# A decoder layer on one core: the next batch's load and transposes moved, identity products in TensorE's waits, work lists laid out anew

## What is computed

```python
x = x + attn(layernorm(x))                  # per batch:
    xs = x shifted by one token
    k, v, r = (x * tm + xs * (1 - tm)) @ W.T, for each of three tm and W; r = sigmoid(r)
    y = (r * layernorm(_wkv(decay, first, k, v)) * ln_g + ...) @ Wo.T
x = x + _wkv(w, u, layernorm(x), ctx)
x = x + ffn(layernorm(x))                   # 1408 inner channels
    h = silu(x @ gate.T * gate_s) * (x @ up.T * up_s)
    y = h @ down.T * down_s
```

## Time and profile before

| | |
|---|---|
| median of three runs | 597.04 us |
| the profiled execution | 597.9 us |
| its span, first to last instruction | 596.1 us |
| mean granted clock of TensorE, share of full speed | 0.958 |
| TensorE busy | 535.3 us, 90% |
| VectorE busy | 458.4 us, 77% |
| ScalarE busy | 350.4 us, 59% |
| GpSimd busy | 52.1 us, 9% |

### The profile page before, as it was taken

How to read it: one execution, slowest core, us unless ns; L and a number is a source line. 1 busy time by engine, 2 the same in 40 slices (tenths; PEclk the granted TensorE clock), 3 DMA queues, 4 the chain that set the end, 5 groups by cost and what they waited for, 6 DMA issues and landing times.

```text
span 596.1 us, 7498 instructions
## 1 busy us (share of the span) xinstructions
PE 535.3 (90%) x2658; PEld 383.0 (64%) x2658; DVE 458.4 (77%) x742; ACT 350.4 (59%) x551; POOL 52.1 (9%) x155
## 2 busy tenths in 40 slices
...
GB/s 304 412 304 369 322 0 0 2 36 35 4 138 2 0 1 0 11 43 19 90 124 1 0 1 0 2 54 18 1 124 2 1 54 36 1 1 36 1 36 38
DMA packets 14264, 39.08 MB, mean 66 GB/s; under 512 B 1233, under 2 KB 1233, under 8 KB 14033
## 3 DMA queue, kind: packets, MB, share of 16 engines
...
...
## 4 chain that ended last, share of the span: by engine, by line
PE 74%; DMA 10%; DVE 7%; issue 3%; SPq 2%; ACT 2%; POOL 2%; DVEq 0%; POOLq 0%; ACTq 0%
PE gu L653 27%; PE bank L569 20%; PE dacc L583 12%; PE bank L631 9%; PE bank L558 5%; DMA down_words<-in_down_t 4%; DMA gate_words<-in_gate_t 3%; DMA t_mixv<-in_x 3%; PE bank L608 1%; DVE t_otile L1076 1%; DVE t_slot L880 1%; DVE t_stats L906 1%; DVE t_z L872 1%; DVE t_st L1018 1%; ACT L676 1%
## 5 line engine op out<-in xcount | busy, mean ns | idle before, releaser
L653 PE MATMUL gu<-t_z4h,t_gate 128*128 128x256 f32 x352 | 93.1, 297 | 1.3 <-DVE t_h L1055 0.7
L653 PE MATMUL gu<-t_z4l,t_gate 128*128 128x256 f32 x352 | 88.5, 284 | 0.0
L653 PE MATMUL gu<-t_z4h,t_up 128*128 128x256 f32 x352 | 87.2, 281 | 0.0
L653 PE MATMUL gu<-t_z4l,t_up 128*128 128x256 f32 x352 | 87.2, 281 | 0.0
L805 ACT ACTIVATE t_h<-gu,t_fsc 128x256 f32<-128x256 f32 x88 | 40.8, 472 | 55.5 <-PE gu L653 50.4
L583 PE MATMUL dacc<-t_down,t_hh 128*128 128x512 f32 x176 | 71.0, 403 | 0.8 <-DVE t_otile L1076 0.8
L653 PEld LDWEIGHTS gu<-t_z4h,t_gate 128*128 128x128 f32 x352 | 67.4, 191 | 6.7 <-issue 3.2
L653 PEld LDWEIGHTS gu<-t_z4l,t_gate 128*128 128x128 f32 x352 | 67.4, 192 | 2.5 <-issue 1.7
L583 PE MATMUL dacc<-t_down,t_hl 128*128 128x512 f32 x176 | 68.9, 391 | 0.0
L676 ACT ACT_TABLE_LOAD x52 | 66.7, 1283 | 1.7 <-PEq L1114 0.7
L653 PEld LDWEIGHTS gu<-t_z4h,t_up 128*128 128x128 f32 x352 | 66.6, 189 | 0.0
(11 more groups left out here) (128 smaller groups left out, 931.1 us busy)
## 6 DMA issues: line engine op xcount, KB each, us to landing
...
gate_words<-in_gate_t SPq DMA_DIRECT2D x1, 2816.0 KB, 17.2
up_words<-in_up_t SPq DMA_DIRECT2D x1, 2816.0 KB, 24.9
t_gate<-gate_words SPq DMA_DIRECT2D x1, 2816.0 KB, 16.4
down_words<-in_down_t SPq DMA_DIRECT2D x1, 2816.0 KB, 23.7
```

The costliest lines, as they stand in the source:

```text
L653: last = pe.matmul(gu[u % 2][:, side, :], as_read(w[:, k, i * P:(i + 1) * P], exact), as_read(part[:, k, hf * HALF:(hf + 1) * HALF], exact ...
```

## The change

Four things. First, `vecs` is loaded behind the two halves of x of batch 0. Second, the copy of the down weights becomes a step of `SP_STEPS` (`copy2.0`), and there x of batch 1 is loaded behind the up weights and ahead of the load of the down weights; the orders of the later loads differ too. Third, a new step `warm` of TensorE issues two products of the identity with itself into a bank that nobody reads at that time; there are eight such steps in the prologue. Fourth, all the lists of steps are new. In batch 0 and 1 `return2.0` now stands ahead of `turn1.1`, `rw0.0` to `rw3.0` ahead of `share_k0.1`, `v3.0` behind `r1.0`, and TensorE's `flag.0` between `r0.1` and `r1.1`. Later `k0`, `k1`, `v0` of batch 2 stand ahead of `wo.1`, `wo.2` ahead of `k0.3`, and `r3.2`, `r3.3` behind `y.1`, `y.2`.

```diff
     PE_STEPS = steps("""
-        turn1.0 k0.0 k1.0 v0.0 v1.0 k2.0 k3.0 v2.0 v3.0 r0.0 r1.0 r2.0 r3.0 turn2.0 turn1.1 k0.1
-        return2.0 k1.1 v0.1 v1.1 wo.0 turn3.0 r0.1 r1.1 r2.1 r3.1 k2.1 k3.1 v2.1 v3.1 y.0 flag.0
-        turn4_0.0 turn4_1.0 up0.0 up1.0 turn2.1 up2.0 up3.0 up4.0 down0.0 return2.1 up5.0 down1.0 up6.0
-        turn1.2 up7.0 wo.1 k0.2 k1.2 v0.2 k2.2 k3.2 up8.0 up9.0 v1.2 v2.2 up10.0 down2.0 up11.0 down3.0
...
-        down16.0 down17.0 up20.0 up21.0 r2.2 r3.2 down18.0 down19.0 down20.0 down21.0 y.1 turn4_0.1
-        turn4_1.1 up0.1 turn2.2 up1.1 up2.1 up3.1 return2.2 down0.1 down1.1 up4.1 turn1.3 up5.1 wo.2
...
-        down16.1 down17.1 down18.1 down19.1 y.2 down20.1 down21.1 r2.3 turn4_0.2 r3.3 up0.2 turn4_1.2
...
+        turn1.0 k0.0 k1.0 v0.0 v1.0 k2.0 k3.0 v2.0 r0.0 r1.0 v3.0 r2.0 r3.0 turn2.0 return2.0 warm0.0
+        warm1.0 turn1.1 warm2.0 warm3.0 k0.1 v0.1 k1.1 v1.1 wo.0 warm4.0 warm5.0 warm6.0 turn3.0 r0.1
+        flag.0 warm7.0 r1.1 r2.1 r3.1 k2.1 k3.1 v2.1 v3.1 y.0 turn4_0.0 turn4_1.0 up0.0 up1.0 turn2.1
+        up2.0 up3.0 up4.0 return2.1 up5.0 down0.0 turn1.2 up6.0 down1.0 k0.2 k1.2 v0.2 wo.1 k2.2 k3.2
...
+        down18.0 down19.0 down20.0 down21.0 y.1 r3.2 turn4_0.1 turn4_1.1 turn2.2 up0.1 up1.1 up2.1
+        return2.2 up3.1 wo.2 up4.1 turn1.3 up5.1 down0.1 k0.3 k1.3 v0.3 v1.3 k2.3 k3.3 down1.1 up6.1
...
+        down19.1 down20.1 down21.1 y.2 r3.3 turn4_0.2 turn4_1.2 up0.2 turn2.3 up1.2 up2.2 up3.2
...
     DVE_STEPS = steps("""
         stat1_0.0 stat1_1.0 norm0.0 norm1.0 mixk0.0 mixk1.0 mixk2.0 mixk3.0 mixv0.0 mixv1.0 mixv2.0
-        front0.0 mixv3.0 mixr0.0 front1.0 nv0.0 den0.0 num0.0 mixr1.0 part0.0 nv1.0 den1.0 num1.0 fin0.0
...
-        part3.0 fin2.0 fin3.0 stat2_0.0 stat2_1.0 stat1_0.1 stat1_1.1 norm2.0 norm3.0 norm0.1 norm1.1
-        mixk0.1 mixk1.1 mixk2.1 mixk3.1 mixv0.1 mixv1.1 front0.1 rw0.0 rw1.0 rw2.0 mixv2.1 mixv3.1 rw3.0
...
+        mixv3.0 mixr0.0 front0.0 front1.0 mixr1.0 mixr2.0 nv0.0 den0.0 num0.0 mixr3.0 part0.0 nv1.0
+        den1.0 num1.0 part1.0 fin0.0 fin1.0 front2.0 front3.0 den2.0 nv2.0 num2.0 part2.0 nv3.0 den3.0
+        num3.0 part3.0 fin2.0 fin3.0 stat2_0.0 stat2_1.0 stat1_0.1 norm2.0 norm3.0 stat1_1.1 norm0.1
+        norm1.1 rw0.0 rw1.0 rw2.0 rw3.0 mixk0.1 mixk1.1 mixk2.1 mixk3.1 mixv0.1 mixv1.1 mixv2.1 mixv3.1
...
+        mixv2.2 mixv3.2 front0.2 den0.2 nv0.2 num0.2 front1.2 rest1.0 prod5.0 rest2.0 x1_0.1 x1_1.1
+        x1_2.1 x1_3.1 part0.2 norm4.1 prod6.0 norm5.1 den1.2 mixr0.2 fin0.2 front2.2 nv1.2 prod7.0
...
+        norm3.2 prod1.1 stat1_0.3 rw0.2 rw1.2 rw2.2 rw3.2 norm0.3 stat1_1.3 x1_0.2 prod2.1 rest0.1
+        prod3.1 norm1.3 x1_1.2 x1_2.2 x1_3.2 rest1.1 norm4.2 norm5.2 mixk0.3 mixk1.3 mixk2.3 mixk3.3
...
     SP_STEPS = steps("""
-        words1.0 words2.0 xload0.1 xload1.1 ctx2.0 ctx3.0 ctx0.1 ctx1.1 rload0.1 rload1.1 xload0.2
...
+        copy2.0 words1.0 xload0.1 xload1.1 words2.0 ctx2.0 ctx3.0 rload0.1 xload0.2 xload1.2 rload1.1
+        xload0.3 ctx0.1 out0.0 ctx1.1 ctx2.1 ctx3.1 out1.0 ctx0.2 out2.0 xload1.3 out3.0 rload0.2 ctx1.2
...
         @block.sync
         def _(sp):
-            sp.dma_start(vecs[:, :, :], vecs_in.rearrange("p (n c) -> p n c", c=C)).then_inc(vec_in, 16)
...
             load_x(0, 0)
             load_x(0, 1)
+            sp.dma_start(vecs[:, :, :], vecs_in.rearrange("p (n c) -> p n c", c=C)).then_inc(vec_in, 16)
...
             copy_words(*ffn_w[0])
             copy_words(*ffn_w[1])
             load_words(*ffn_w[0])
-            copy_words(*ffn_w[2])
...
+                elif s == "copy2":
+                    copy_words(*ffn_w[2])
...
+                elif kind(s) == "warm":
+
+                    for _ in range(2):
+                        pe.matmul(gu[1][:, 0, 0:P], ident[:, :], ident[:, :], start=True, stop=True)
```

More of the change, by code:

```diff
@@ L124, in decoder_layer @@
[L124 to L125 removed]
+        share_v3.0 share_r0.0 share_r1.0 share_r2.0 front0.0 share_r3.0 front1.0 part0.0 part1.0
+        front2.0 front3.0 tanh0.0 tanh1.0 part2.0 tanh2.0 part3.0 tanh3.0 weigh0.0 weigh1.0 norm2.0
+        norm3.0 norm0.1 norm1.1 rw0.0 rw1.0 rw2.0 rw3.0 share_k0.1 share_k1.1 share_k2.1 share_k3.1
@@ new lines, in decoder_layer @@
+        share_v0.1 share_v1.1 share_v2.1 share_v3.1 share_r0.1 share_r1.1 share_r2.1 share_r3.1 weigh2.0
+        front0.1 front1.1 weigh3.0 weigh4.0 part0.1 part1.1 sq4.0 sq5.0 norm4.0 norm5.0 xfront0.0
+        xfront1.0 weigh5.0 xpart0.0 xpart1.0 xfront2.0 xfront3.0 tanh0.1 tanh1.1 tanh2.1 tanh3.1
+        xpart2.0 xpart3.0 front2.1 front3.1 sq6.0 sq7.0 norm6.0 norm7.0 z4_0_0.0 z4_0_1.0 part2.1
+        z4_1_0.0 z4_1_1.0 part3.1 silu0.0 silu1.0 silu2.0 high0.0 norm2.1 norm3.1 silu3.0 high1.0
@@ new lines, in decoder_layer @@
+        high7.0 xpart1.1 silu18.0 silu19.0 xfront2.1 xfront3.1 high8.0 high9.0 silu20.0 silu21.0
+        xpart2.1 high10.0 tanh0.2 xpart3.1 tanh1.2 tanh2.2 sq6.1 sq7.1 norm6.1 tanh3.2 z4_0_0.1 norm7.1
+        z4_0_1.1 z4_1_0.1 z4_1_1.1 silu0.1 norm2.2 norm3.2 silu1.1 silu2.1 rw0.2 rw1.2 rw2.2 high0.1
+        rw3.2 silu3.1 sq4.2 norm0.3 norm1.3 high1.1 sq5.2 share_k0.3 share_k1.3 share_k2.3 share_k3.3
+        share_v0.3 share_v1.3 share_v2.3 share_v3.3 silu4.1 silu5.1 front0.3 front1.3 part0.3 norm4.2
@@ L134, in decoder_layer @@
-        mixr0.1 front1.1 nv0.1 den0.1 nv1.1 num0.1 part0.1 den1.1 num1.1 mixr1.1 part1.1 x1_0.0 x1_1.0
-        x1_2.0 fin0.1 x1_3.0 norm4.0 fin1.1 norm5.0 mixr2.1 mixr3.1 xfront0.0 xfront1.0 xin0.0 xin1.0
-        xden0.0 xnum0.0 xpart0.0 xden1.0 xnum1.0 xpart1.0 xfin0.0 xfront2.0 xfin1.0 xin2.0 xfront3.0
-        xden2.0 xnum2.0 xpart2.0 xin3.0 xden3.0 xnum3.0 xpart3.0 xfin2.0 xfin3.0 front2.1 front3.1
-        den2.1 nv2.1 nv3.1 num2.1 xf_0.0 xf_1.0 xf_2.0 xf_3.0 weigh.0 part2.1 den3.1 flag.0 norm6.0
```

152 lines of the change are left out of this document (70 added, 82 removed).

## The result

The changed kernel takes **594.34 us** (median of seven runs, 592.88 to 595.06); the kernel before, on the same chip, 596.83. The ratio is **0.9956** (95% interval 0.9944 to 0.9969), so it is faster by 2.6 us. The forecast was 586.7, a gain of 10.3: the sign is right, three quarters of the gain are missing, and the time sits just inside the upper end of the range. The profiled execution took 594.34 itself (span 592.5, mean granted clock 0.968).

A forecast was written before the change was run, and what follows sets the result against it. TensorE, busy 535.3 of 596.1 us, bounds the kernel, nearly tied with VectorE between 206.5 and 296.9. Gains 6.0 + 0.5 + 2.4 + 1.5 = 10.4 off 597.9 give 587.5, by the median 586.7; range 581.5 to 594.5.

The forecast's parts named there:

- parts 1 to 5: Prologue, from the first loads to x1_3.0 and turn3.0: 6.0 us gained by x1_3.0 and 0.5 for turn3.0.
- Part 1: Start of batch 0: `vecs` lands behind x, so first statistics come at 8.1 instead of 5.37, 2.7 us later; bounds 0 to 3.5.
- Part 3: x of batch 1, loaded ahead of the down weights, lands at 64.7 and 66.1 instead of 72.03; 1.7 of 4.6 us stall gained.
- Part 4: return2.0 ahead of turn1.1: share_k0.1 0.65 us earlier, 4.7 leave the line behind it, 0.65 from clock; 6.0 by x1_3.0.
- Part 5: Sixteen identity products in prologue waits, 0.4 us each: 0 on the path, at worst +1.2; clock gain 0.5 for turn3.0.
- The third case: Rival: identity products hold the clock in every hole, so turn2.0, return2.0 and turn1.1 run fast; 15 us gain, 582; chance 0.12.
- Part 6: From x1_3.0 to up0.0: no gain, as VectorE is busy 39.7 of 41.1 us and has the same work.
- Part 7: Lists after 172 us: r3.2 behind `y.1` gains 2.4 net and 1.5 of clock; later passes 0, from -2 to +2.
- only the prologue pays: Rival: VectorE's busy stretch before 297 pins xfin3.1 and the clock falls as before, so only 6.0 us gained, 591; chance 0.20.
- The falling signs: Forecast falls if share_k0.1 comes after 82, first statistics stay at 5.4, or new `t_mixk`, `t_h`, `t_z` waits exceed 3 us.
- The slower rival: x1_2 and x1_3 set inside VectorE's bound stretch delay scans, xfin3, y and the next up; 13 us lost, 600; chance 0.09.

The follow-up runs named there:

- The twelfth kernel: New lists up to `up0.0`, old lists behind, `vecs` loaded first, plus r3.2 moved behind `y.1` and tanh3.2 behind norm6.1: 589.55 us, ratio 0.9857 to the kernel before.
- the third kernel: The changed kernel with `vecs` loaded ahead of x of batch 0 again: 590.25 us, ratio 0.9874 to the kernel before.

## Why the prediction was right and wrong

**The prologue, parts 1 to 5: right, 6.5 forecast, 6.04 measured at `up0.0`.** Part 1's order of landing (x, then `vecs`) is confirmed, and so are its 2.7 us (2.7 at the first statistics, 2.4 at the first scan); the profiles with `vecs` first are 2.6 to 3.2 us earlier at `up0.0`, near the upper bound of 3.5. Part 3's landing in time and the price left of the move (later readings of return2 ahead of share_k0.1) came out within 0.3 us. What the working did not see is how the sum divides. It credited the load with 1.7 of the 4.6 us stall; alone the load is worth 6.9, because the late x also swallows a head start in batch 0. Part 4, which carried 4.7 of the 6.0, takes out what it said behind k0.1 (4.8 us) and puts 4.0 of it back ahead of k0.1, so that it is worth 0.7 to 1.6 with everything else of the prologue beside it, and the runs can't tell it from the other small edits. That the two parts add up to the forecast is partly luck.

**Part 5: right in size, wrong in place.** The products are worth about 0.9 us (not clear of noise), forecast 0.5, and cost nothing on the path (k0.1 starts at 81.26 with them and 81.18 without). Four took 1.26 and 1.57 us, 0.3 to 0.4 each, as estimated. The gain is at k0.1, not at turn3.0 where the 0.5 was counted. "turn1.1's last rows as fast more likely than not" held in seven of ten profiles and not in the one of the changed kernel. The third case (the clock holds in every hole) is refuted by return2.0's sixteen transposes in 3.87 us. The Trainium skill ("TensorE: Matmul & The Clock Gate", What's actually happening) ties the rate to whether the array was busy. The rows agree as far as they go: behind an idle stretch of 4.74 us return2.0 ran at half rate, and k0.1 met the full clock with the products ahead of it (1.00) and half where TensorE had waited instead (0.50).

**Part 6: right**; `up0.0` comes where the sum put it. What no part had: the old lists take 141.05 us from `up0.0` to `up1.1` in the kernel before and 139.49 behind the new prologue. Of the difference 0.7 is `up0.0`, which no longer starts at half clock, and 0.8 is `up0.1`, where the full clock came back sooner. So the new lists' own loss in the first pass is 1.7 us (141.20 against 139.49) and not the ledger's 0.15.

**Part 7 is the step that failed: 3.9 us of gain forecast, 3.1 of loss measured in the ledger, 7.0 of the 7.6 us by which the number was off (0.5 more is the prologue's).** Its two halves failed differently.
- *The first pass.* "TensorE then reaches y.1 3.4 us sooner, and VectorE must have ended xfin3.1 sooner too" took VectorE's idle 10 us ahead of 206.5 for a reserve. It was not one. VectorE did the same 109 us of work in the same 125, its idle time only came later, inside the waits for wo.1's banks and ScalarE, and TensorE's work moved out of the stretch turned into new waits for `t_h`. The twelfth kernel shows it alone: VectorE's chain sets `up0.1`, and of the filled hole (2.4) and the full clock (1.5) next to nothing is paid out. The rival "only the prologue pays" had this reason, at 591, and was given 0.20, with the very row that decides it, 87.4 of 90.4 us.
- *The later passes.* A gain of "0, from -2 to +2" was a loss of 2.9 (275.69 us before and 278.63 after from `up1.1` to the last step). The step named what was thinned out, r3.3 alone behind `y.2`, and priced it rightly at 2 us of cover (2.0 in the third kernel, at full clock), then set it off against "fewer waits before it". There were hardly any to win before it (113.41 against 113.65), and the halved clock in `turn4_1.2`, `up0.2` and `turn2.3` came on top with another 2.0. The clock was counted where the change helps (`y.1`) and not where the same edit hurts (`y.2`); and it comes by execution: with this order it cost between 0 and 2.0 us in six profiles.

The falling signs that the prediction set, new waits for `t_h`, `t_mixk` or `t_z` behind 172 us of over 3 us together, are what the profile shows (2.3 us for `t_h` in three waits, and 2.1 for `t_z` at `y.2` alone). The slower rival (x1 steps in VectorE's bound stretch) had the right engine for the first pass only, and priced the later steps at 13 us against the forecast, where some 8 are measured: the 3.9 did not come, and the new lists behind `up0.0` are slower by 4.0 to 4.3 us, hidden in the sum by the prologue.
